# Order of two groups of transposes on TensorE in the expert slots of an attention and mixture-of-experts kernel

## What is computed

```python
logits = xf @ router_w.T                      # xf: layer norms of x, 2048 x 256
probs = softmax(logits)                       # 8 experts
topk_p, topk_i = top_k(probs, 2)
for eid in range(8):
    xe = xf * dense_gate[:, eid:eid + 1]
    gate, up = split(xe @ gate_up_w[eid].T)   # 256 -> 2 x 512
    hidden = silu(gate) * up
    out = out + hidden @ down_w[eid].T        # 512 -> 256
x = x + tanh(g_ffn) * out
```

## Time and profile before

| | |
|---|---|
| median of 3 runs | 546.45 us (544.29 to 546.94) |
| the profiled execution | 547.43 us |
| its span, first to last instruction | 545.1 us |
| PE busy in the span | 511.6 us (94%), 3712 matmuls |
| weight loads (PEld) | 475.5 us (87%) |
| DVE, ACT, POOL busy | 340.2, 290.6 and 213.3 us |
| mean granted TensorE clock | 0.985 |

### The profile page before, as it was taken

How to read it: one execution, slowest core, us unless ns; L and a number is a source line. 1 busy time by engine, 2 the same in 40 slices (tenths; PEclk the granted TensorE clock), 3 DMA queues, 4 the chain that set the end, 5 groups by cost and what they waited for, 6 DMA issues and landing times.

```text
span 545.1 us, 11962 instructions
## 1 busy us (share of the span) xinstructions
PE 511.6 (94%) x3712; PEld 475.5 (87%) x3712; DVE 340.2 (62%) x811; ACT 290.6 (53%) x881; POOL 213.3 (39%) x242
## 2 busy tenths in 40 slices
PE   7899999999999999999999798989889999999992
PEld 6698999999999999999998687877778888888881
DVE  5956676667768778587685777578745563333330
ACT  3446666656555556456655565576346654444341
POOL 5063100305604569318374168335423343332332
PEclk9999999999999999999998989999999999999997
DMA  8700000499991011100023066554386653343421
GB/s 232 239 0 2 1 1 2 140 304 297 288 290 62 0 39 38 39 0 10 31 78 99 0 207 190 123 134 116 79 240 167 138 78 46 54 60 58 59 30 20
DMA packets 50418, 54.35 MB, mean 100 GB/s; under 512 B 8832, under 2 KB 46464, under 8 KB 50368
## 3 DMA queue, kind: packets, MB, share of 16 engines
q1 hardware_dynamic: 43216, 44.38, 28.5%
q0 software_dynamic: 7152, 9.33, 10.8%
HBM read 24.12 MB, written 29.58 MB: 99 GB/s over the span
## 4 chain that ended last, share of the span: by engine, by line
PE 67%; DVE 12%; issue 6%; DMA 4%; ACT 3%; DVEq 2%; POOLq 2%; POOL 2%; SPq 1%; ACTq 0%
PE bank L914 13%; PE bank L739 9%; PE bank L685 8%; PE bank L763 8%; PE bank L701 8%; PE bank L934 6%; PE bank L715 5%; DMA out_dram<-yq,tok 2%; PE bank L748 2%; PE bank L924 2%; PE bank L859 2%; PE bank L659 1%; DVE nmax L1213 1%; PE bank L782 1%; DVEq L1171 1%
## 5 line engine op out<-in xcount | busy, mean ns | idle before, releaser
L1022 ACT ACTIVATE probs<-bank,nmax 128x154 f32<-128x154 f32 x256 | 98.3, 395 | 81.6 <-DVE nmax L1213 81.6
L602 POOL DMA_INDIRECT out_dram<-yq,tok x39 | 60.8, 1560 | 119.2 <-ACT yq L1101 57.9
L739 PE MATMUL bank<-vdiag,pT 128*128 128x128 f32 (+2 forms) x640 | 79.8, 272 | 1.0 <-DVE oT_lo L1237 0.6
L739 PEld LDWEIGHTS bank<-vdiag,pT 128*128 128x128 f32 (+1 forms) x640 | 77.6, 194 | 1.7 <-DVE oT_lo L1237 1.1
L1213 DVE TENSOR_REDUCE nmax<-bank 128x2 f32<-128x308 f32 x128 | 57.0, 476 | 34.1 <-PE bank L701 33.9
L914 PE MATMUL bank<-gu_hi,xqT_hi 128*128 (+1 forms) x156 | 67.9, 435 | 0.0
L914 PE MATMUL bank<-gu_lo,xqT_hi 128*128 (+1 forms) x156 | 61.5, 394 | 0.0
L914 PE MATMUL bank<-gu_hi,xqT_lo 128*128 (+1 forms) x156 | 61.3, 393 | 0.0
L1580 DVE TENSOR_TENSOR hidT_lo<-bank,hidT_hi 128x512 fp32r<-128x512 f32 x39 | 26.9, 690 | 47.0 <-ACT hidT_hi L1094 46.7
L1575 DVE TENSOR_TENSOR hid<-hid,bank 128x512 f32<-128x512 f32 x39 | 26.8, 687 | 43.1 <-PE bank L914 42.9
L1022 ACT ACTIVATION_READ_ACCUMULATOR probs<-bank,nmax 128x1 f32 x256 | 53.2, 208 | 0.0
(11 more groups left out here) (211 smaller groups left out, 1323.6 us busy)
## 6 DMA issues: line engine op xcount, KB each, us to landing
expert_queue<-zrow SPq DMA_DIRECT2D x8, 2184.5 KB, 23.0
gu_raw<-in_gate_up_wT_dram SPq DMA_DIRECT2D x16, 512.0 KB, 4.3
xq<-expert_queue SPq DMA_DIRECT2D x39, 128.0 KB, 2.9
dn_raw<-in_down_wT_dram SPq DMA_DIRECT2D x8, 512.0 KB, 4.3
x<-in_x_dram SPq DMA_DIRECT2D x4, 512.0 KB, 13.2
out_dram<-out SPq DMA_DIRECT2D x8, 256.0 KB, 4.6
wq_raw<-in_L_xattn_Wq_dram SPq DMA_DIRECT2D x1, 1024.0 KB, 11.7
wo_raw<-in_L_xattn_Wo_dram SPq DMA_DIRECT2D x1, 1024.0 KB, 10.4
```

What stands on the lines that cost most here:

```text
L602: nc.gpsimd.indirect_dma_start(out[:, :], bass.IndirectOffsetOnAxis(tok[j % (2 * RT)][:, 0:1], 0), yq[p][:, :], None, compute_op=ALU.add). ...
L739: last = nc.tensor.matmul(at[:, col0 + j0 * DH:col0 + j0 * DH + n], pT[u % 2][0:rows, b, :], v, start=(b == 0), stop=(b == NBLK - 1), skip ...
L1022: last = nc.scalar.activation(probs[u % 4][:, j * NKB:(j + 1) * NKB], S_BANK[hf][:, m * NKB:(m + 1) * NKB], ACT.Exp, bias=nmax[:, u % 4, j ...
```

## The change

In slot j the two transposes of the rows of tile j + 1 stand right behind the four transposes of `hid`, ahead of the gate projection; before, they stood between the gate and the up projection. In slot 3, `turn_features(NI, 1)` stands ahead of the transposes of `hid` and not behind them. Nothing is added or taken away, and no wait is changed; the waits of the moved steps move with them.

```diff
                     rank = rank_of(i, p)
                     tile_before = (i - 1, RT - 1) if p == 0 else (i, p - 1)
-                    transpose_hidden(*tile_before)
                     if j == 3:
                         turn_features(NI, 1)
+                    transpose_hidden(*tile_before)
+                    if more:
+                        transpose_rows(i + (p + 1) // RT, (p + 1) % RT)
                     up(i, p, rank, 0, G_BANK, "e_gate", "e_silu")
                     if j == 2:
                         turn_features(NI, 0)
@@
                     if j == COUNT_SLOT:
                         rows_before(NI)
-                    if more:
-                        transpose_rows(i + (p + 1) // RT, (p + 1) % RT)
                     up(i, p, rank, 1, U_BANK, "e_up", "e_hid")
```

## The result

| | before | after |
|---|---|---|
| median of the runs beside each other (22 each) | 546.15 us | 548.87 us |
| ratio after to before, 95% interval | | 1.005 (1.0034 to 1.0065) |
| profiled execution, its span | 547.43, 545.1 us | 549.14, 546.8 us |
| mean granted TensorE clock | 0.985 | 0.986 |

The changed kernel is slower by 0.5%, 2.7 us between the medians. The forecast was 548.2 us; the time lies inside its range, on the slow side.

A forecast was written before the change was run, and what follows sets the result against it. TensorE's own pace was taken to bound slots from about 13 on, waits for DVE and row loads slots 2 to 12. Terms -0.42 + 0.69 + 1.48 = +1.75 us on the 546.45 us median gave 548.2 us, range 545.2 to 550.8.

The forecast's parts named there:

- Ordinary slots, 0 ± 0.5 us: Some 25 slots from about 13 on: the pair costs 0.21 us in either place, so 0, within 0.5 us in all.
- change-over rival: First matmul behind transposes costs 0.09 us; one such place per slot goes: -3.2 us over 36 slots, 545.0 us; chance 0.10.
- Slot 2, 0 us: Tile 3's rows land a little late, but 1.17 us of idle time waiting for DVE covers it: 0.
- late-load rival: The load of tile 3 comes late by a gate projection, its cover gone: +1.4 us, 549.6 us; chance 0.08.
- Slot 3, -0.42 us: Feature transposes fill idle time, 0.21 us; the up projection loses the pair ahead of it, 0.21 us more: -0.42 us.
- Slot 10, +0.69 us: The pair now waits for tile 11's rows ahead of the gate projection; up projection later by 0.69 us (0.45 to 1.25).
- the landing: Slot 10: tile 11's rows, issued at 387.80, were taken to let the first transpose start at 390.15 us.
- Slot 12, +1.48 us and the carried delay: Gate projection now stands behind the wait for tile 13's rows: +1.48 us, plus 0.69 us brought along from slot 10.
- nothing behind it takes this back: Behind slot 12 the ordinary slots have no wait left, so the loss there reaches the end whole.
- clock rival: Some 2.8 us of idle time in slot 12 makes TensorE's clock fall: +2.5 us, 550.7 us; chance 0.12.
- The delay carried by the load of tile 13: Tile 13's load queues behind slot 10's output blocks, so it moves with that slot's up projection, by 0.69 us.
- Rival 3: Loads of tiles 11 and 13 come early enough that neither exposure arises; only slot 3's gain is left: 546.0 us; chance 0.12.

The follow-up runs named there:

- slot 3 alone: Kernel before with the changed order only in slot 3, feature transposes ahead of the hid transposes: 546.31 beside 545.24 us, ratio 1.0012.
- slot 10 alone: Kernel before with the row transposes moved ahead of the gate projection only in slot 10: 546.71 beside 545.79 us, ratio 1.0014.
- slot 12 alone: Kernel before with the row transposes moved only in slot 12, run twice: 548.52 beside 545.79 us and 547.77 beside 544.91 us.
- the two repeats: The changed kernel timed twice more against the kernel before: 548.54 beside 545.24 us and 549.54 beside 544.91 us.
- filled kernels: Changed kernel, twice, and its move in slot 12 only, each plus 32 unused matmuls there: 548.28, 548.41, 546.75 us; ratios to before 1.0044, 1.0068, 1.0043.

## Why the prediction was right, and where its sizes were off

**Ordinary slots, 0 ± 0.5 us: right.** 4.86 us in both kernels; over the 25 slots from 13 to 37 the changed kernel is 0.19 us shorter, 0.008 us per slot. The pair costs the same in either place, and the change-over rival falls. No row load came late behind slot 13.

**Slot 2, 0 us: right, its cover thin.** The load of tile 3 came late by 0.25 us, and the wait for DVE absorbed it, as the step said. The late-load rival asked for 1.4 us, so it falls too.

**Slot 3, -0.42 us: right.** -0.39 at slot 4, and the same at slot 10, so the chain of slots 4 to 9 passed it on whole; the kernel with slot 3 alone shows the same.

**Slot 10, +0.69 us: right in mechanism, too small.** It measured +1.05 us in the changed kernel and +0.87 alone. The mis-sized term is the landing. It was taken at 390.15, that is 57.57 us in the count of the table above. In the kernel with slot 10 alone the pair starts at 386.60 - 328.83 = 57.77, 0.20 us later, about as much as the whole difference (the pair's own 0.07 us more is given back by the end of the slot). In the changed kernel the gain of slot 3 should have brought it to 57.15; it starts at 388.90 - 331.48 = 57.42, since the issue moved ahead by only (387.80 - 332.58) - (386.39 - 331.48) = 0.31 us and the landing took 2.51 us instead of the 2.35 taken. The rest is the pair itself: 389.26 - 388.90 = 0.36 us to the next matmul, where 0.14 was read from a busy stretch (0.20 or 0.21 us in four other profiles with the pair behind this wait). The gate projection behind it took its 1.48 us (390.74 - 389.26). So the up projection is 0.27 + 0.22 = 0.49 us later than the sum had it, and the end of the slot made up 0.1 of that.

**Slot 12, +1.48 us and the carried delay: right in mechanism, and incomplete.** Slot 12 became 2.49 us longer. By the table of slot 12 that is 4.48 - 3.13 = 1.35 us for the gate projection that now stands behind the wait (the term of 1.48), 6.06 - 4.48 = 1.58 us for the clock, and 2.77 - 3.21 = -0.44 us for the wait, in which two things meet: the load was issued 0.37 us later against the start of the slot, and was there 3.55 us behind its issue instead of 4.36. The step "nothing behind it takes this back" held: of +3.15 at slot 13, +2.94 reached the end. What failed is the chance of 0.12 for the clock rival: the fall was in all five profiles with the wait ahead of the gate projection and no fillers. The prediction leaned on the 2 us of idle time between 384 and 388 us in the earlier trace rows, which left the clock at 1.00 in both kernels, and carried it on to a longer piece that no row showed; 2.14 us and more went the other way. It also read that the clock had fallen once. In the same profile it had fallen another time, from 293.7 to 297 us, and the profile shows no idle piece of TensorE between 287.96 and that fall; one of the stretches there:

```profile
294.00:295.00 1.00, 1.00 (x6) 1.00 (x6) 0.03 (x1) 0.00 (x0) 0.10 (x1) 0.50 0.09 16
```

So the clock had fallen even where no idle piece stands in the profile, which speaks against taking 2 us of it as proof of safety. The price of 2.5 us was high for four of five profiles. The Trainium skill states this rule in "TensorE: Matmul & The Clock Gate" (section "HAM oscillation — how this bites in real kernels"): a wait for DMA amid matmul work lets the clock fall, and the next work starts slow. These traces agree for the five waits of 2.14 to 3.19 us, at 1.4 to 2.7 us each, and not for those of 0.71 to 1.18 us, behind which the clock stayed at 1.00; the waits in the page's example are longer than the 2.8 us that the prediction priced, so its "by that page" claimed more than the page does.

**The delay carried by the load of tile 13.** It was taken to come along rigidly. Against the profile of before it didn't: with slot 10 alone, slot 12 starts 0.91 us late and the pair only 70.69 - 70.03 = 0.66. But with slot 12 alone, where nothing is carried, the pair comes 0.28 to 0.30 us earlier than before. Against those two the pair with slot 10 alone is 0.95 us later. SP's issue of this load shows the carry without the landing; the first row is from slot 10 alone, the second from slot 12 alone:

```profile
395.74 0.37 SPq L182 DMA_DIRECT2D xq<-expert_queue  x1
```

```profile
397.80 0.37 SPq L182 DMA_DIRECT2D xq<-expert_queue  x1
```

Counted from slot 1 the issue comes at 398.25 - 332.58 = 65.67 in the profile of before and at 397.80 - 332.13 = 65.67 with slot 12 alone, but at 395.74 - 328.83 = 66.91 with slot 10 alone and at 398.18 - 331.48 = 66.70 in the changed kernel. These are 1.24 and 1.03 us later, where slot 12 itself starts 0.91 and 0.66 us later. So the delay was carried, and in SP's queue, where the output blocks ahead of the load moved by only 0.86 and 0.65 us, it grew: against the start of slot 12 the load comes 0.33 and 0.37 us later, a term that the prediction doesn't have. All profiles agree: the issue lies 0.75 to 0.82 us ahead of the start of slot 12 in the six with slot 10 moved, and 1.14 to 1.20 us in the eight without. Why it grew, no run here tells. The profile of before had an unusually slow landing: 4.36 us from issue to pair, against 3.88 to 4.06 in the six other profiles with slot 10 unmoved and a wait in slot 12. The step from hid transposes to pair takes 2.70 to 3.81 us in the profiles with the early pair.

**The sum.** From the profiles, without the clock and with the wait of slot 12 taken as equal: -0.39 + 1.05 + 1.35 - 0.2 = +1.8 us, where +1.75 was forecast; that the two meet is luck, the terms' errors cancel. With the time from issue to landing taken as equal instead, the later issue adds its 0.37: +2.2 us. The times say +2.7 us (1.9 to 3.6 by the interval), and the two repeats 3.3 and 4.6 between the medians. The difference is of the size that the clock costs in the profiles. But the filled kernels, whose profiles lack the fall, also took 3.0 and 3.5 us more than before between the medians, while their profiles end their last slot 2.03 and 1.44 us late; +2.2 lies inside the interval of the first (1.1 to 3.8 us) and just under that of the second (2.4 to 5.0). What makes up that remainder isn't settled. The start of the expert part alone varies from 328.8 to 332.6 us among the profiles, more than the terms in question, and the clock has a part in this: over 305 to 325 us, where the attention ends, it is 1.00 in three profiles, which start slot 1 at 328.8, 328.8 and 330.6 us, 0.83 in ten, which start it at 329.9 to 332.6, and 0.91 in one (331.7).

**Rival 3**, no exposure, falls with the two waits of 0.71 and 2.14 us.

## What to carry to other kernels

Before moving a step that waits for a transfer ahead of independent work, look for the few places where its transfer is already late: there the work that it overtakes joins the wait in full, while in the slots without such a wait the move changed nothing here. The useful move at a wait is the opposite one, more independent work ahead of it, and it may be made for one slot only; here it gave 0.25%. A wait that empties TensorE must be priced with the slow stretch that can follow it: a shorter piece of idle time that left the clock alone says little of a longer one.

## What the runs showed of the hardware that wasn't expected

- The granted clock stayed at 1.00 over the 2.05 us of idle time that ended at 385.89 and fell to 0.50 behind the 2.14 us that ended at 401.73, in one execution. What sets the two apart besides the 0.09 us, no run here tells. Nor did the work's return set the moment: in the second profile of the changed kernel the clock was at 0.91 over 402:403, with PE still empty up to 403.83, and with slot 12 alone it was at 0.80 over the same microsecond, with PE back at work since 401.86.
- In the profile of before the clock stood at 0.50 over 294:297 without a wait that the profile shows: TensorE's last idle piece had ended at 287.96, and ahead of the fall stood transposes and matmuls of 64 and 8 columns, sixteen of them in the 1.95 us from 291.38.
- At 0.50 the same matmuls of 512 columns are 0.43 us apart instead of 0.23. The low stretch lasted some 3.5 us behind 2.14 us of idle time and over 6 us behind 3.19 us (at 0.50 from 403 to 409).
- Thirty-two matmuls without any use, 1.95 us in an otherwise empty stretch, kept the clock at 1.00 and delayed nothing behind them in that slot.
